# Turning the row maxima of an attention kernel with an fp32r product in place of an fp32 transpose

## The chip, the core and the metric

The kernel runs on one core of one Trainium2 chip. The time is the device time of one execution in microseconds (us); smaller is better. The engines of the core are TensorE (PE, with its weight loads shown apart as PEld), VectorE (DVE), ScalarE (ACT), GpSimd (POOL) and SyncE (SP), and each works through its own instructions in order.

## What is computed

A block of cross attention with 16 heads of width 64, followed by a mixture of 8 experts of which each token uses 2. The first argument of the attention (`x` inside it) is the context, 154 rows; the latents are the normalised `x`, 512 rows. The queries come from the latents, keys and values from both, 154 + 512 = 666 rows. Batch 2, width 128.

```python
def _L0_xattn_ref(x, latents, ln_m_g, ln_m_b, ln_l_g, ln_l_b, Wq, Wkv, Wout):
    x = layer_norm(x, ln_m_g, ln_m_b)
    lat = layer_norm(latents, ln_l_g, ln_l_b)
    q = lat @ Wq
    kv = jnp.concatenate([x, lat], axis=1) @ Wkv
    k, v = jnp.split(kv, 2, axis=-1)            # then split into 16 heads
    dots = jnp.einsum('bhid,bhjd->bhij', q, k) * scale
    attn = jax.nn.softmax(dots, axis=-1)
    out = jnp.einsum('bhij,bhjd->bhid', attn, v)
    return out @ Wout

x = x + _L0_xattn_ref(ctx_1024, _layernorm(x), ...)
x = x + _L0_ffn_ref(_layernorm(x), ...)         # 8 experts, top 2, hidden 256
```

## The kernel before

The order of all work is written out by hand, engine by engine, and semaphores tie the engines together. All operands live in the core's own memory; only weights are loaded on the way.

**Steps.** Attention runs in 16 steps `s`, one for each pair of heads and batch. The scores are held transposed: keys on the partitions (6 tiles of 111 keys, `kt` = 0 to 5), queries along the 512 columns. The softmax needs for each query the maximum over its keys, and this is found a step ahead on scores that are the other way round: `lead` makes them (queries on the partitions), `reduce_max` on VectorE takes the negated maxima of each of six units, and `join_max` joins them into `neg_max`, 2 heads of `TURN` = 64 columns, of which the first four of each head are used and the rest stay zero. `neg_max` is thus a tile of 128 by 128, with a query on each partition.

**The turn.** `turn_max` (line 343) turns this tile on TensorE: `neg_max` is the stationary operand and the identity `ident` streams through, 128 columns. The result stands in a bank of `sc`. `spread_max` on VectorE (line 782) multiplies it by a selection `sel` and writes `max_row` in fp32r; the last two products of each score tile (line 368) multiply `max_row` by ones, which subtracts the maximum from the scores. ScalarE then takes the exponential (`exponent`, line 636).

**Order on TensorE in a step** (lines 466 to 504): six rounds of `dots(s, kt)` (lines 362 and 368) with `lead_next(s + 1, kt)` behind each (line 326); the projections of q and k for step s + 2; half of a projection of v (`project_v`, lines 295 to 297, 9 products of 256 columns); `turn_max(s + 1)`; `total(s - 1)`, the softmax sums of the step before (line 389); and 24 records of `pv(s, kt)` (line 382). Step 14 has a part of the output projection (`out_project`, line 460) where the others have that of v, and step 0 has no `total`. `turn_max(0)` runs once ahead of the steps, behind the first half of `project_v(0)`.

**fp32 and fp32r.** An operand declared fp32r has 32 bits but is rounded to fewer digits by whoever writes it. Products of such operands stand in the trace as one record; ordinary fp32 products (lines 382, 389, 460, 564) stand there as two. The transposes of fp32 tiles (lines 345, 407, 410, 513, 530) stand there as one record. The trace prints both types as f32 on TensorE.

**GpSimd** builds `ident` and `sel` at the start (lines 972 to 987), then waits for the variances of the inputs (`rstd_of`, line 1000); in the steps it adds the exponentials up (`gather`, line 1050).

Of the kernel before, what the change touches and what calls it, by code (L numbers as in the profile page):

```python
# [15 lines left out]
F32 = mybir.dt.float32  # L16
F32R = mybir.dt.float32r
# [4 lines left out]
P = 128  # L22
# [19 lines left out]
TURN = 64  # L42
# [27 lines left out]
def xattn_moe(nc, x, ctx_in, g_m, b_m, g_l, b_l, wq, wkv, wout, wg, w1, b1, w2, b2, out):  # L70
    with ExitStack() as stack:
        def sb(name, shape, dt=F32):
            return stack.enter_context(nc.sbuf_tensor(name, shape, dt))
# [4 lines left out]
        def sem(name):  # L78
            return stack.enter_context(nc.semaphore(name))
# [4 lines left out]
        rows = sb("rows", [E * HC + 4, P])  # L84
        cols = sb("cols", [P, E * HC + 4])
        ident = sb("ident", [P, P])
        sel = sb("sel", [P, QT])
        sel2 = sb("sel2", [P, 2, QT])
        ones = sb("ones", [P, HD])
# [18 lines left out]
        k_pair = sb("k_pair", [P, QKB, 2, J], F32R)  # L108
        v_sb = sb("v_sb", [P, 2, KT, 2 * P])
        part_max = sb("part_max", [P, 2, 2, QT])  # L110
        neg_max = sb("neg_max", [P, 2, TURN])
        max_row = sb("max_row", [P, 2, N], F32R)
        probs = sb("probs", [P, RING, 2, N])
        psum_acc = sb("psum_acc", [P, 2, 2, N])
# [40 lines left out]
        tail_loaded = sem("tail_loaded")  # L155
        consts = sem("consts")
        sel_ready = sem("sel_ready")
        ones_ready = sem("ones_ready")
        cols_turned = sem("cols_turned")
        cols_ready = sem("cols_ready")  # L160
# [30 lines left out]
        neg_turned = sem("neg_turned")  # L191
# [101 lines left out]
        def _(pe):  # L293
# [48 lines left out]

            def turn_max(n, bank=sc[:, 1, 1, :]):
                pe.wait_ge(neg_ready, n + 1)
                pe.transpose(bank[:, 0:P], neg_max[:, :, :].rearrange("p h c -> p (h c)"), ident[:, :]) \
                  .then_inc(neg_turned, 1)

            def dots(s, kt):
                if kt == 0:
# [99 lines left out]
            pe.wait_ge(kv_ready, 2 * B)  # L449
            project_v(0, 0, sc[:, 0])  # L450
            turn_max(0, mx[:, 0, :])
            pe.wait_ge(v_copied, 1)

# [12 lines left out]
            for s in range(STEPS - 1):  # L466
# [21 lines left out]
                if v_half(s):  # L488
# [5 lines left out]
                    else:  # L494
                        project_v(*v_half(s))
                pe.wait_ge(exp_done, s * KT + KT)
                turn_max(s + 1)
                if s >= 1:
                    total(s - 1)
# [227 lines left out]
        def _(dve):  # L727
            own = [0]

            def chained(op):  # L730
                op.then_inc(setup_v, 1)
                own[0] += 1
                dve.wait_ge(setup_v, own[0])
# [62 lines left out]
                dve.reciprocal(at, at).then_inc(recip_done, 1)  # L796

            chained(dve.memset(moments[:, :, :, :], 1.0))
            dve.memset(neg_max[:, :, :], 0.0)

            def input_tiles(b):
                return [(t, x_tok[:, b, t, :]) for t in range(QT)] + \
# [168 lines left out]
        def _(pool):  # L971
# [13 lines left out]

            pool.wait_ge(consts, 3)
            pool.tensor_tensor(sel[:, :], sel2[:, 0, :], sel2[:, 1, :], ALU.add).then_inc(sel_ready, 1)

            def split_qk(p):
                pool.wait_ge(wqk_loaded[p % 2], 32 * (p // 2 + 1))  # L990
                if p >= 2:
                    pool.wait_ge(k_lo_done, 2 * (4 * (p // 2 - 1) + p % 2 + 2) + 2)
                pool.tensor_copy(wqk_hi[:, p % 2, :, :], wqk_raw[:, p % 2, :, :]).then_inc(wqk_hi_ready, 1)
                pool.wait_ge(wqk_hi_ready, p)
                pool.tensor_tensor(wqk_lo[:, p % 2, :, :], wqk_raw[:, p % 2, :, :],
                                   wqk_hi[:, p % 2, :, :].bitcast(F32), ALU.subtract).then_inc(wqk_split, 1)
# [114 lines left out]
```

## Time and profile before

| | us |
|---|---|
| median of 3 runs | 356.56 (356.44 to 356.78) |
| the profiled execution | 356.89 |
| its span, first to last instruction | 355.1 |
| TensorE busy | 342.6 (96%) |
| VectorE, GpSimd, ScalarE busy | 240.2, 240.7, 181.2 |

The span is what the trace covers; the profiled execution lasted 1.8 us longer than its span. TensorE's records overlap: the next product starts while one drains, so that the time a product costs is read from the start of one record to the start of the next, not from its duration. The weight loads (PEld) run ahead of the products that use them.

### The profile page before, as it was taken

The page shows a single profiled execution, that of the slowest core. Times are in us where ns is not written, and L with a number is a line of the kernel's source. Part 1 is how long each engine was busy: PE and PEld are TensorE (multiplying, and loading weights), DVE is VectorE, ACT ScalarE, POOL GpSimd, SP SyncE. Part 2 cuts the span into 40 slices and gives each one's busy share as a digit, 9 for nine tenths or more (in the row PEclk, how much of TensorE's full clock was granted, in tenths as well). Part 3 has the DMA queues.
Part 4 walks back from the last instruction along what each step waited for, and adds up shares of the span by engine and source line. Part 5 has one row for each costly group of instructions (what it writes and reads, how often), then busy time and mean ns, then how long its engine had stood idle before and what let it go on. Part 6 is the DMA issues. An engine that isn't in the chain of part 4 may idle for free.

```text
span 355.1 us, 6060 instructions
## 1 busy us (share of the span) xinstructions
PE 342.6 (96%) x2343; PEld 231.0 (65%) x2343; DVE 240.2 (68%) x418; ACT 181.2 (51%) x240; POOL 240.7 (68%) x160
## 2 busy tenths in 40 slices
PE   2879999999999999999999999999999999999996
PEld 2758574656657474756556474747584559999986
DVE  4789286878677686868686776968744488257433
ACT  2247383755648383836556383838433553135341
POOL 3577586979797989999798989779695661010000
PEclk9999999999999999999999999999999999999999
DMA  3044000000001010010100000000000000000000
GB/s 122 0 145 124 2 14 2 2 2 0 2 0 31 0 31 15 2 30 2 30 3 16 0 2 2 0 2 0 2 0 2 1 0 3 2 0 2 30 2 30
DMA packets 6713, 5.81 MB, mean 16 GB/s; under 512 B 743, under 2 KB 5789, under 8 KB 6685
## 3 DMA queue, kind: packets, MB, share of 16 engines
q1 hardware_dynamic: 6389, 5.29, 5.0%
q8 instruction: 19, 0.31, 0.3%
q10 hardware_dynamic: 296, 0.13, 0.1%
q14 instruction: 9, 0.07, 0.1%
HBM read 4.89 MB, written 0.52 MB: 15 GB/s over the span
## 4 chain that ended last, share of the span: by engine, by line
PE 94%; DVE 3%; DMA 1%; ACT 1%; ACTq 1%; issue 0%; DVEq 0%
PE xo L382 23%; PE sc L362 20%; PE mx L564 8%; PE sc L368 6%; PE sc L295 5%; PE xo L389 5%; PE sc L297 4%; PE sc L296 4%; PE mx L326 3%; PE xo L326 3%; PE mx L460 2%; PE xo L460 2%; PE mx L295 2%; PE mx L297 2%; PE mx L296 2%; DVE part_max L767 1%
## 5 line engine op out<-in xcount | busy, mean ns | idle before, releaser
L1050 POOL TENSOR_TENSOR psum_acc<-psum_acc,probs 111x1024 f32<-111x1024 f32 x63 | 150.0, 2380 | 7.2 <-DVE psum_acc L790 2.5
L636 ACT ACTIVATE probs<-sc 111x1024 f32<-111x1024 f32 x96 | 98.3, 1027 | 21.3 <-PE sc L368 13.9
L362 PE MATMUL sc<-q_pair,k_pair 64*111 64x512 f32 x576 | 85.7, 401 | 1.0 <-ACT v_sb L626 0.8
L382 PE MATMUL xo<-probs,v_sb 111*64 111x512 f32 x384 | 85.6, 593 | 0.0
L362 PEld LDWEIGHTS sc<-q_pair,k_pair 64*111 64x111 f32 x576 | 44.6, 170 | 28.4 <-issue 12.2
L767 DVE TENSOR_REDUCE part_max<-mx 128x2 f32<-128x888 f32 x32 | 34.7, 1084 | 41.0 <-PE mx L326 39.6
L382 PEld LDWEIGHTS xo<-probs,v_sb 111*64 111x64 f32 x384 | 27.3, 137 | 53.6 <-issue 53.2
L796 DVE RECIPROCAL recips<-recips 128x128 f32<-128x128 f32 x64 | 54.3, 910 | 9.4 <-ACT recips L646 9.4
L1050 POOL TENSOR_TENSOR psum_acc<-probs 111x1024 f32<-111x1024 f32 x16 | 38.4, 2398 | 30.7 <-ACT probs L636 30.7
L640 ACT COPY o_t<-xo 128x512 f32<-128x512 f32 x16 | 9.4, 588 | 66.6 <-PE xo L382 66.6
L368 PE MATMUL sc<-max_row,ones_r 64*111 64x512 f32 x192 | 38.1, 390 | 0.0
L703 ACT ACTIVATE probs<-sc,cols 128x512 f32<-128x512 f32 x32 | 21.5, 687 | 28.3 <-PE sc L297 28.0
L767 DVE TENSOR_REDUCE part_max<-xo 128x2 f32<-128x888 f32 x30 | 32.5, 1084 | 1.4
L941 DVE SCALAR_TENSOR_TENSOR x_tok<-mx,score,x_tok 128x128 f32<-128x128 f32 x62 | 17.5, 344 | 22.1 <-PE mx L564 21.9
L564 PEld LDWEIGHTS mx<-w_sb,probs 128*128 128x128 f32 x248 | 29.9, 192 | 2.0 <-issue 0.8
L564 PE MATMUL mx<-w_sb,probs 128*128 128x128 f32 x248 | 30.2, 275 | 0.0
L1057 POOL TENSOR_TENSOR o_t<-o_t,recips 128x512 f32<-128x512 f32 x16 | 20.5, 1278 | 11.2 <-DVE recips L796 11.2
L368 PEld LDWEIGHTS sc<-max_row,ones_r 64*111 64x111 f32 x192 | 16.9, 170 | 5.5
L326 PE MATMUL mx<-k_pair,q_pair 64*128 64x444 f32 (+1 forms) x128 | 18.3, 320 | 1.3 <-DVE part_max L767 0.5
L771 DVE TENSOR_REDUCE part_max<-mx 128x4 f32<-128x888 f32 x16 | 17.3, 1082 | 1.4
L626 ACT COPY v_sb<-mx 111x768 f32<-111x768 f32 x15 | 12.0, 799 | 12.0 <-PE mx L297 12.0
L389 PE MATMUL xo<-psum_acc,ones 111*64 111x512 f32 x64 | 17.3, 618 | 0.0
(169 smaller groups left out, 478.9 us busy)
## 6 DMA issues: line engine op xcount, KB each, us to landing
w_raw<-in_L_ffn_W SPq DMA_DIRECT2D x8, 128.0 KB, 2.0
x_tok<-in_x SPq DMA_DIRECT2D x2, 256.0 KB, 3.4
wv_raw<-in_L_xattn_Wkv SPq DMA_DIRECT2D x4, 128.0 KB, 2.8
wout_sb<-in_L_xattn_Wout SPq DMA_DIRECT2D x1, 512.0 KB
wqk_raw<-in_L_xattn_Wq SPq DMA_DIRECT2D x7, 64.0 KB, 2.0
wqk_raw<-in_L_xattn_Wkv SPq DMA_DIRECT2D x7, 64.0 KB, 2.0
out<-x_tok SPq DMA_DIRECT2D x1, 256.0 KB, 2.0
out<-x_tok SPq DMA_DIRECT2D x2, 128.0 KB, 1.7
```

Of the source, the lines that this page charges most:

```text
L295: pe.matmul(out_ap, st_hi, mv_hi, start=True, stop=False)
L326: mm = pe.matmul(to, q_pair[r, n % QKB, 0, t * P:(t + 1) * P], k_pair[r, n % QKB, 0, k_cols(u >= QT)], start=True, stop=True)
L362: pe.matmul(sc[0:KP, kt % 2, h, :], k_pair[r, s % QKB, k_part, at], q_pair[r, s % QKB, q_part, :], start=(k_part + q_part == 0), stop=False)
L368: mm = pe.matmul(sc[0:KP, kt % 2, h, :], ones_r[r, :], max_row[r, s % 2, :], start=False, stop=True)
L382: mm = pe.matmul(o_ps[h * HD:(h + 1) * HD, :], v_sb[0:KP, s // 2 % 2, kt, at:at + HD], probs[0:KP, e % RING, h, :], start=(kt == 0), stop= ...
L389: mm = pe.matmul(bank[h * HD:(h + 1) * HD, :], ones[0:KP, :], psum_acc[0:KP, s % 2, h, :], start=True, stop=True)
L564: mm = pe.matmul(y_ps(g, t)[:, t * P:(t + 1) * P], relu_ring[:, (g * HC + c) % FR, t * P:(t + 1) * P], w2_sb[:, e * HC + c, :], start=(c = ...
L636: act.activation(probs[0:KP, e % RING, :, :], sc[0:KP, kt % 2, :, :], ACT.Exp).then_inc(exp_done, 1)
L703: act.activation(relu_ring[:, n % FR, :], hid_ps[:, n % 4, :], ACT.Relu, bias=cols[:, n % (E * HC):n % (E * HC) + 1]).then_inc(relu_done, 1)
L767: dve.tensor_reduce(part_max[:, 0, :, u], banks[:, :, 0:KW], AX.X, ALU.max, negate=True) \
L796: dve.reciprocal(at, at).then_inc(recip_done, 1)
L1050: pool.tensor_tensor(psum_acc[0:KP, s % 2, :, :], first, probs[0:KP, e % RING, :, :], ALU.add) \
```

## The change

`neg_max` is declared fp32r, a copy `ident_r` of the identity in fp32r is made by GpSimd at the start, and `turn_max` becomes a plain product of the two. The first turn also waits for `ident_ready`. VectorE's clearing of `neg_max` writes the same bits through an fp32 view. No instruction changes its place; GpSimd gets one more.

```diff
@@ -84,6 +84,7 @@
         ident = sb("ident", [P, P])
+        ident_r = sb("ident_r", [P, P], F32R)
@@ -108,7 +109,7 @@
-        neg_max = sb("neg_max", [P, 2, TURN])
+        neg_max = sb("neg_max", [P, 2, TURN], F32R)
@@ -342,8 +344,10 @@
             def turn_max(n, bank=sc[:, 1, 1, :]):
                 pe.wait_ge(neg_ready, n + 1)
-                pe.transpose(bank[:, 0:P], neg_max[:, :, :].rearrange("p h c -> p (h c)"), ident[:, :]) \
-                  .then_inc(neg_turned, 1)
+                if n == 0:
+                    pe.wait_ge(ident_ready, 1)
+                pe.matmul(bank[:, 0:P], neg_max[:, :, :].rearrange("p h c -> p (h c)"), ident_r[:, :],
+                          start=True, stop=True).then_inc(neg_turned, 1)
@@ -796,7 +800,7 @@
-            dve.memset(neg_max[:, :, :], 0.0)
+            dve.memset(neg_max[:, :, :].bitcast(F32), 0.0)
@@ -985,6 +989,7 @@
             pool.tensor_tensor(sel[:, :], sel2[:, 0, :], sel2[:, 1, :], ALU.add).then_inc(sel_ready, 1)
+            pool.tensor_copy(ident_r[:, :], ident[:, :]).then_inc(ident_ready, 1)
```

## Rows read from the trace of the kernel before

**Rows 1.** The page: busy time of each engine, and shares of the last chain.
```profile
PE 342.6 (96%) x2343; PEld 231.0 (65%) x2343; DVE 240.2 (68%) x418; ACT 181.2 (51%) x240; POOL 240.7 (68%) x160
...
PE 94%; DVE 3%; DMA 1%; ACT 1%; ACTq 1%; issue 0%; DVEq 0%
```
**Rows 2.** Timeline of TensorE around one turn: start us, us, engine, line, operation, xcount.
```profile
66.49 0.27 PE L295 MATMUL sc<-kv_hi,wqk_hi 128*128 128x222 f32 x1
66.60 0.27 PE L296 MATMUL sc<-kv_lo,wqk_hi 128*128 128x222 f32 x1
...
67.76 0.29 PE L297 MATMUL mx<-wv_hi,kv_lo 128*111 128x256 f32 x1
67.88 0.27 PE L345 MATMUL sc<-ident,neg_max 128*128 128x128 f32 x1
68.09 1.08 PE L389 MATMUL xo<-psum_acc,ones 111*64 111x512 f32 x4
69.00 5.32 PE L382 MATMUL xo<-probs,v_sb 111*64 111x512 f32 x24
74.25 0.95 PE L362 MATMUL sc<-q_pair,k_pair 64*111 64x512 f32 x6
```
**Rows 3.** Line 345: its loads and products, ns min/median/max, and who waited for them.
```profile
L345 PEld LDWEIGHTS sc<-ident,neg_max x15: 138/140/144, 34.8 to 265.4; 128*128 128x128 f32 x15
L345 PE MATMUL sc<-ident,neg_max x15: 270/272/274, 34.9 to 265.6; 128*128 128x128 f32 x15
...
  DVE max_row L782: 9.0, 16
```
**Rows 4.** Waits of the whole span: engine, line, releaser: us in total, times, longest.
```profile
ACT o_t L640 <- PE xo L382: 66.6, 16, 4.6
...
DVE part_max L767 <- PE mx L326: 39.6, 15, 7.0
POOL psum_acc L1050 <- ACT probs L636: 30.7, 16, 4.3
...
PEld sc L362 <- ACT probs L636: 7.2, 36, 0.6
```
**Rows 5.** Timeline: a v product of 256 columns, then the 64-wide tiles of line 382.
```profile
38.84 0.28 PE L297 MATMUL mx<-wv_hi,kv_lo 128*111 128x256 f32 x1
39.05 0.20 PEld L382 LDWEIGHTS xo<-probs,v_sb 111*64 111x64 f32 x4
39.05 0.65 PE L382 MATMUL xo<-probs,v_sb 111*64 111x512 f32 x2
```
**Rows 6.** Timeline: an expert's product of 512 columns, then line 389.
```profile
290.74 0.40 PE L297 MATMUL sc<-kv_hi,w_lo 128*128 128x512 f32 x1
...
291.06 0.65 PE L389 MATMUL xo<-psum_acc,ones 111*64 111x512 f32 x2
```
**Rows 7.** Timeline: a transpose of 77 columns, then the half-height tiles of line 326.
```profile
20.77 0.23 PE L410 MATMUL sc<-ident,normed 77*128 77x77 f32 x1
20.92 0.37 PE L326 MATMUL sc<-k_pair,q_pair 64*128 64x222 f32 x2
```
**Rows 8.** Timeline: 128-column loads and products of 8 columns, eight of each.
```profile
287.18 0.97 PEld L521 LDWEIGHTS mx<-wg_sb,kv_t 128*128 128x128 f32 x8 [0.81 <-ACT kv_t L697]
287.18 1.06 PE L521 MATMUL mx<-wg_sb,kv_t 128*128 128x8 f32 x8
```
**Rows 9.** Timeline of the weight loads: fp32r loads of 128 columns at 222-column products.
```profile
14.99 0.19 PEld L296 LDWEIGHTS sc<-kv_lo,wqk_hi 128*128 128x128 f32 x1
15.10 0.19 PEld L297 LDWEIGHTS sc<-kv_hi,wqk_lo 128*128 128x128 f32 x1
```
**Rows 10.** Timeline: the join of the maxima, and the load and spread that use it.
```profile
66.33 0.17 DVE L777 TENSOR_REDUCE neg_max<-part_max 128x8 f32<-128x16 f32 x1
...
68.19 0.69 DVE L782 TENSOR_TENSOR max_row<-sc,sel 128x512 fp32r<-128x512 f32 x1 [0.25 <-PE sc L345]
...
67.76 0.14 PEld L345 LDWEIGHTS sc<-ident,neg_max 128*128 128x128 f32 x1
```
**Rows 11.** Timeline of the first turn.
```profile
23.31 0.27 PE L345 MATMUL mx<-ident,neg_max 128*128 128x128 f32 x1
23.51 0.80 ACT L626 COPY v_sb<-sc 111x768 f32<-111x768 f32 x1 [0.77 <-PE sc L297]
23.69 0.69 DVE L782 TENSOR_TENSOR max_row<-mx,sel 128x512 fp32r<-128x512 f32 x1 [0.78 <-PE mx L345]
...
24.36 0.71 PE L362 MATMUL sc<-q_pair,k_pair 64*111 64x512 f32 x4 [0.78 <-ACT v_sb L626]
```
**Rows 12.** Timeline of GpSimd at the start, and the group of its 256-column casts.
```profile
2.19 0.20 POOL L987 TENSOR_TENSOR sel<-sel 128x4 f32<-128x4 f32 x1
6.99 1.34 POOL L1000 TENSOR_TENSOR rstd<-var_eps,half_power 128x6 f32<-128x6 f32 x1 [4.59 <-DVE var_eps L808]
...
L993 POOL CAST wqk_hi<-wqk_raw 128x256 fp32r<-128x256 f32 x7 | 2.8, 399 | 2.2 <-DVE normed L746 2.2
```
**Rows 13.** The chain that ended last, in order of time: start us, us, what.
```profile
348.76 1.80 PE mx L564 x16
350.56 0.02 issue
350.58 1.14 DVE x_tok L941 x4
```

More of the change, by code:

```diff
@@ L157, in xattn_moe @@
         sel_ready = sem("sel_ready")
+        ident_ready = sem("ident_ready")
         ones_ready = sem("ones_ready")
```

## The prediction

> **What bounds the kernel now.** I read the page's shares first: TensorE is busy for 96% of the span and makes 94% of the chain that ended last, so a step is worth what it takes of TensorE's time from start to start, if the rest follows [rows 1]. Does it follow? In the waits, the long ones all point at TensorE or at something it drives: ScalarE waits 66.6 us for line 382, VectorE 39.6 us for line 326, GpSimd 30.7 us for the exponentials, each about once a step [rows 4]. No engine is full in a step and none keeps a pace of its own. TensorE's own waits inside the steps are the 36 short ones for exponentials, 7.2 us together [rows 4]; they are waits for a ScalarE that itself started from TensorE's scores, so they move with it. Behind the turn I see no wait at all: line 389 follows the turn at once, its 4 records and the 24 of line 382 run through to the next step's scores at 74.25 [rows 2]. At the end, TensorE works until 350.56 and VectorE adds up behind it [rows 13]. So time taken off a turn in a step should come off the end, one for one.
>
> The turn itself: line 345 is one record a turn, 15 in the steps and one ahead of them, 272 ns long with a load of 140 ns [rows 3]. What it costs is not 272 ns. It starts at 67.88 and line 389 starts at 68.09 (the same place of other steps gives 0.20): 0.20 us [rows 2]. That is the term of the sum, 15 times 0.20 us = 3.0 us, under 1% of the kernel, and the change can only take a part of it.
>
> **What the 0.20 us is made of.** The next product loads 64-wide tiles where the turn used the full array, and its load starts only with it. Every such switch in the trace shows the streaming of the last product plus about 0.1 us. A 256-column v product (fp32r) before line 382: 39.05 - 38.84 = 0.21 [rows 5]. A 512-column one before line 389: 291.06 - 290.74 = 0.32 [rows 6]. The difference is 0.11 us for 256 columns, 0.43 ns a column, and leaves 0.10 us for the switch. An fp32 transpose of 77 columns before another switch: 20.92 - 20.77 = 0.15 [rows 7]; with the turn's 0.20 at 128 columns that makes 0.05 us for 51 columns, some 0.8 to 1 ns a column. So a transposed fp32 column costs about twice an fp32r column, and the switch costs about the same 0.1 us behind both.
>
> **The change, part by part.** The product: 128 columns at 0.43 ns are 0.055 us, plus 0.10 for the switch: 0.155 us from the turn to line 389 where it was 0.20. Bounds: going down from the 512-column row, 0.32 - 384 x 0.42 ns = 0.16, with rounding 0.165; going from the 77-column transpose, whose stream was about 0.065, 0.15 - 0.065 + 0.055 = 0.14. So 0.045 us a turn, between 0.035 and 0.06. I take the middle because the 256-column row is nearest in kind: the same engine mode before, the same 64-wide fp32 tiles behind.
>
> No row has an fp32r product narrower than 222 columns. Those start 66.60 - 66.49 = 0.11 us apart [rows 2], which is still 0.43 ns a column and some 10 ns; whether 128 columns keep that rate is the unknown of this case.
>
> The load: a transpose loads 128 columns in 0.14 us [rows 3], an fp32r product in 0.19 [rows 9], 0.05 longer. Eight loads of 128 columns with products of only 8 columns start in 0.97 us, that is (0.97 - 0.19) / 7 = 0.11 us apart [rows 8], so such a load needs 0.11 us of the array's load path. It starts with the product before, which streams 256 columns and holds the turn back by 67.88 - 67.76 = 0.12 us anyway [rows 2]. The 222-column products hold loads of this size with 0.11 between them [rows 2, 9]. I cost it at nothing; the cover is that v product (in step 14 the output projection's last), and without it up to 0.05 us a turn would come back.
>
> The trace shows a transpose as a single record, and not as the two of an ordinary fp32 product, so the turn had no fourfold cost to lose. The Trainium skill says the same against this change ("TensorE: Matmul & The Clock Gate", Terms): transpose mode is 4x faster for FP32. By that rule the old turn would already stream at the fp32r rate and the change would gain nothing; rows 2 and 7, with 0.8 to 1 ns a column, say it is about half that fast, which no other row contradicts. It is the first rival below.
>
> The join on VectorE writes 8 fp32r elements instead of 8 fp32 ones. It ends at 66.50 and the load that needs it starts at 67.76 [rows 10]: 1.26 us of cover, and the other steps look alike. The spread starts about 0.04 us earlier, and nothing waits for that: its result is needed in the next step's line 368, over 5 us later [rows 2, 10].
>
> The first turn: behind it TensorE waits for ScalarE's copy of v, which ends at 24.31, and not for the turn [rows 11]. Gain and cost there: nothing. Its additional wait is for a copy on GpSimd at about 2.4 us. That copy is 128 columns, less than the 0.40 us of a 256-column cast, say 0.3; GpSimd then waited 4.59 us for VectorE's variances, so it is hidden too [rows 12]. The first turn comes at 23.31, so the wait is long fulfilled.
>
> **The sum.** 15 turns x 0.045 = 0.68 us; with the bounds 0.5 to 0.9. The profiled execution lasted 356.89, 0.33 over the median; the gain is a difference and carries over: 356.56 - 0.68 = 355.88. The three runs shown spread over 0.34 us. About 0.2% of this time, 0.71 us, is what a measurement can tell from no change, so the forecast lies just inside it, and its upper half outside.
>
> **The rivals.**
>
> *Nothing comes back (0.20).* Either the transpose already streams as fast as fp32r, or the longer load shows: 0.045 gained and up to 0.05 lost, or the gain is caught by a wait of ScalarE or GpSimd later in the step. Each gives 0 to 0.35 us, 356.2 to 356.6. Against: rows 7 against 2 for the rate, rows 8 for the load, rows 4 for the waits. For: 0.01 us of rounding in rows from which 0.045 is taken. The Trainium skill's section on the back-to-back gap (the same page) gives about 81 ns for a pair of load and 128-column product, as an estimate 0.03 us more than streaming alone; by it 0.02 us a turn and 0.3 us in all are gained.
>
> *Slower (0.10).* The fp32r rate does not hold for narrow products. If a product below some width between 128 and 222 columns falls back to what an ordinary fp32 one takes, it costs as two records of line 564: 16 records took 1.80 us [rows 13], 0.11 each, 0.22 for the product. From turn to line 389 that is 0.32 instead of 0.20, 15 x 0.12 = 1.8 us, time 358.4. The 222-column products show no sign of such a fall, which is why it gets little. It decides as soon as a 128-column stream costs over 0.10 us, what the transpose pays now. Half a fall, two cycles a column, would be no change.
>
> *More than the sum (0.05).* The switch is shorter behind an fp32r stream of this width, or a wait for exponentials goes too: 1.0 us or more, 355.5 or less.
>
> **Chances.** The forecast case, 0.5 to 0.9 us, has 0.65: of it 0.34 shows as faster by over 0.2% and 0.31 as within, since the sum lies just inside the bound and the medians scatter by 0.1 us or so. With the large gain faster has 0.39; with the first rival within has 0.51; slower has 0.10. The range goes from 355.6, the upper bound of the gain with some scatter, to 356.6, no gain at all; left out are the slow rival and a part of the large gain.
>
> **What would show it.** In the changed kernel's timeline the turn should start 0.12 behind the v product as before, and line 389 (393 in the changed file) 0.15 to 0.16 behind the turn; the product's duration falls from 272 to about 230 ns, its load rises from 140 to about 190. The distance between two turns, 16.2 us, should fall by 0.045. If the turn starts later behind the v product, the load shows. If the gap is 0.3, narrow fp32r products are slow. If the gap falls but the distance of turns doesn't, a wait in the scores' rounds took it.

## The result and the profile after

| | before | after |
|---|---|---|
| median, us (22 runs each) | 356.63 (356.37 to 357.10) | 356.19 (355.83 to 356.51) |
| profiled execution, us | 356.89 | 356.11 |
| its span, us | 355.1 | 354.4 |

The ratio is 0.9986, with a 95% interval from 0.9980 to 0.9992: 0.44 us or 0.14% less, a gain by its interval, and under the 0.2% that the prediction took as the least that a measurement can tell. In us the interval is 0.29 to 0.71. The forecast was 355.9 in a range from 355.6 to 356.6. In some executions of either kernel, though in none of these 44, TensorE's granted clock falls for a while near the start and the time is 1 to 2 us longer (last section); medians called "at full clock" below leave those out.

The turn in the changed kernel, in the timeline of TensorE (start us, us, engine, line, operation, xcount), answers to [rows 2]:

```profile
67.40 0.28 PE L299 MATMUL mx<-wv_hi,kv_lo 128*111 128x256 f32 x1
67.52 0.22 PE L349 MATMUL sc<-ident_r,neg_max 128*128 128x128 f32 x1
67.67 0.65 PE L393 MATMUL xo<-psum_acc,ones 111*64 111x512 f32 x2
```

It starts 0.12 us behind the v product, as it did, and line 393 (389 before) starts 0.15 behind it where it was 0.20. The instructions of the new line, with min/median/max in ns and the first and last start, answer to [rows 3]:

```profile
L349 PEld LDWEIGHTS sc<-ident_r,neg_max x15: 187/188/192, 34.4 to 264.7; 128*128 128x128 f32 x15
L349 PE MATMUL sc<-ident_r,neg_max x15: 218/221/305, 34.6 to 264.7; 128*128 128x128 f32 x15
...
  DVE max_row L786: 8.1, 16
```

The load is 0.05 us longer and the product 0.05 us shorter, about as forecast. The starts tell where the time went: in the timeline, from the second turn to the sixteenth it is 264.73 - 34.55 = 230.18 us, against 265.56 - 34.87 = 230.69 before. That is 14 steps, and 0.51 us less.

The busy time and the waits say nothing new, which is a result too; they answer to [rows 1] and [rows 4]:

```profile
PE 341.0 (96%) x2343; PEld 231.9 (65%) x2343; DVE 240.1 (68%) x418; ACT 181.3 (51%) x240; POOL 241.1 (68%) x161
...
ACT o_t L644 <- PE xo L386: 66.6, 16, 4.6
...
DVE part_max L771 <- PE mx L328: 39.5, 15, 7.0
POOL psum_acc L1055 <- ACT probs L640: 30.0, 16, 4.2
```

The copy of the identity, 0.29 us, sits in GpSimd's idle time at the start, and the join writes fp32r in the 171 ns that it took before (the first two rows are from the timeline, the last from the groups by shape; they answer to [rows 10, 12]):

```profile
2.34 0.29 POOL L992 CAST ident_r<-ident 128x128 fp32r<-128x128 f32 x1
7.08 1.34 POOL L1005 TENSOR_TENSOR rstd<-var_eps,half_power 128x6 f32<-128x6 f32 x1 [4.45 <-DVE var_eps L812]
...
L781 DVE TENSOR_REDUCE neg_max<-part_max 128x8 fp32r<-128x16 f32 x16 | 2.7, 171 | 0.6
```

So the turns gave 15 x 0.05 = 0.75 us, and 0.44 arrived by the medians. The upper end of the interval, 0.71, is close to 0.75, so the times alone don't prove that anything is missing; the steps of the trace do, for this one execution (next section). The question for the experiments was where that part stayed, and whether it is the narrow fp32r product, the type or the mode that makes a turn cheap.

### The profile page after: what moved, and what is told of

Its sections match the earlier page's. It is cut to its first block, busy times and chain, and to the rows that moved or that the text cites. A ratio compares the mean times of both kernels' runs of the same rounds, so it can differ in the third digit from the quotient of the medians.

```text
span 354.4 us, 6062 instructions
## 1 busy us (share of the span) xinstructions
PE 341.0 (96%) x2343; PEld 231.9 (65%) x2343; DVE 240.1 (68%) x418; ACT 181.3 (51%) x240; POOL 241.1 (68%) x161
## 4 chain that ended last, share of the span: by engine, by line
PE 92%; DVE 4%; ACT 1%; DMA 1%; ACTq 1%; issue 0%; DVEq 0%
PE xo L386 23%; PE sc L366 20%; PE mx L568 8%; PE sc L372 6%; PE sc L297 5%; PE xo L393 5%; PE sc L299 4%; PE sc L298 4%; PE mx L328 3%; PE xo L328 3%; PE mx L464 2%; PE xo L464 2%; PE mx L297 2%; PE mx L298 2%; PE mx L299 2%; DVE part_max L771 1%
## 5 line engine op out<-in xcount | busy, mean ns | idle before, releaser
L640 ACT ACTIVATE probs<-sc 111x1024 f32<-111x1024 f32 x96 | 98.3, 1027 | 21.6 <-PE sc L372 14.8
```

Source lines behind the costliest of these rows:

```text
L640: act.activation(probs[0:KP, e % RING, :, :], sc[0:KP, kt % 2, :, :], ACT.Exp).then_inc(exp_done, 1)
```

## A measure for the steps

The gain per step is 0.05 us, and single executions of one kernel lie up to 0.7 us apart. The trace is finer: from the turn to the sums it is 200 to 204 ns in each of the eleven steps used here of the kernel before. Whole steps differ more (16211 to 16272 ns in the same trace), so their mean carries some 5 ns of scatter (from their spread, an estimate). For each kernel I took the mean over the eleven steps from the third turn to the fourteenth, in which the work is the same, and split it: from the turn to the sums or, where the turn is several records, from the first of them; the rounds of the scores, numbered from 0 as `kt` is, each from its first product to that of the next round; the whole step. Two of the rounds are shown. In ns:

| kernel | turn to sums | round 2 | round 4 | step |
|---|---|---|---|---|
| before | 202 | 1181 | 1178 | 16235 |
| changed, the profile above | 150 | 1193 | 1202 | 16205 |
| changed again (e6) | 150 | 1175 | 1190 | 16188 |
| changed again (e12) | 149 | 1177 | 1188 | 16186 |
| all but the product (e3) | 202 | 1180 | 1179 | 16236 |
| transpose of fp32r data (e5) | 151 | 1177 | 1175 | 16178 |
| the same again (e11) | 151 | 1180 | 1177 | 16178 |
| 192 columns (e7) | 178 | 1182 | 1186 | 16231 |
| 256 columns (e1) | 207 | 1179 | 1181 | 16242 |
| 512 columns (e8) | 320 | 1178 | 1182 | 16357 |
| plain fp32 product (e4) | 313 | 1176 | 1184 | 16344 |
| four fp32r products (e9) | 485 | 1179 | 1197 | 16525 |
| four fp32r transposes (e10) | 385 | 1179 | 1188 | 16428 |

The piece from the sums to the first round is 6159 ns in every row. In the changed kernel's first profile rounds 2 and 4 are 12 and 24 ns longer than before and round 3 is 9 ns shorter, 27 ns in all; small differences elsewhere bring that to the 22 ns that are missing between the 52 ns off the turn and the 30 ns off the step. Rounds 2 and 4 are those which TensorE starts soonest behind the exponential that frees their bank: about 0.10 us behind its end, and 0.15 us in rounds 3 and 5.

## The experiments

**e1 and e8: a longer turn.** The changed kernel with a wider identity, whose further columns are zeros and write columns that nobody reads; every turn but the first streams 256 or 512 columns. In the diffs from here on, `...` stands for what is cut; here GpSimd's clearing of the further columns, and the wait of the first turn for it, are cut too.

```diff
-        ident_r = sb("ident_r", [P, P], F32R)
+        ident_r = sb("ident_r", [P, 256], F32R)          # or 512, 192
-                pe.matmul(bank[:, 0:P], neg_max..., ident_r[:, :],
+                wide = 256 if n else P
+                pe.matmul(bank[:, 0:wide], neg_max..., ident_r[:, 0:wide],
```

For 256 columns:

> The changed kernel, but from step 0's turn on the fp32r identity is 256 columns wide (the upper 128 are zeros and write columns nobody reads), so that the turn streams as long as an fp32 transpose should. From turn to line 389 0.21 us where the changed kernel has 0.15. Theory A (whatever a turn costs more or less reaches the end one for one): 15 x 0.055 = 0.8 us over the changed kernel, 357.0 us. Theory B (about a third of it is taken back by the rounds of the scores, as in the changed kernel, where 0.75 us came off the turns and 0.44 us off the time): 0.5 us over it, 356.7 us, no difference from the kernel before.

Measured: median 356.90 against 356.74 for before on the same chip, ratio 1.0005 (0.9988 to 1.0023); the interval holds both theories. For 512 columns there are two entries. In the first, six executions took 877.83, 1203.34, 360.59, 358.39, 358.44 and 358.79 us. The profiled one is the 877.83, so its trace isn't used here (last section); the 360.59 has the clock's fall of that section too, and the last three are at full clock and lie nearer to theory A's 358.7 than to 357.9.

> The same with 512 columns. From turn to line 389 0.32 us, 0.17 more than in the changed kernel, 15 times: 2.5 us. Theory A (one for one): 358.7 us. Theory B (two thirds arrive): 357.9 us. It also shows whether the rate of 0.43 ns a column holds from 128 to 512 columns.

The second was made for the trace:

> The 512-column identity again, since the execution that was profiled the first time was a disturbed one. From turn to line 389 0.32 us. Theory A (one for one above the changed kernel's 0.15): step 16.205 + 0.17 = 16.375 us; if a third is taken back, 16.32. Theory C: 16.35 to 16.37, because the kernel with plain fp32 products, 0.11 us longer than before, has passed on 0.11 of it.

Its time was 358.66, 1.65 over the 357.01 of before on that chip. The turn in the timeline, for 256 and then for 512 columns:

```profile
51.13 0.28 PE L350 MATMUL sc<-ident_r,neg_max 128*128 128x256 f32 x1
51.34 1.08 PE L394 MATMUL xo<-psum_acc,ones 111*64 111x512 f32 x4
```

```profile
51.74 0.40 PE L350 MATMUL sc<-ident_r,neg_max 128*128 128x512 f32 x1
52.06 1.08 PE L394 MATMUL xo<-psum_acc,ones 111*64 111x512 f32 x4
```

0.21 and 0.32 us to the next product, with 0.15 at 128 columns: (0.32 - 0.15) / 384 = 0.44 ns a column and 0.09 us for the switch. That is the line that the prediction had drawn from 256 and 512 columns, and it holds down to 128. On the path: the 512-column turn is 118 ns longer than the transpose and the step is 122 longer; 5 ns and 7 with 256 columns. Measured from the kernel before, everything arrives where a turn gets longer. Against theory B it is the 512 columns that speak: by it the step should be 16.32 us, and it is 16.357; theory A, drawn from the 16.205 of the changed kernel's first profile, had 16.375, and theory C's 16.35 to 16.37 holds it. e1 can't decide: its turn is as long as that of before, so theory B has the step of before for it, which came (16242 against 16235).

**e7: 192 columns**, the same edit.

> The identity is 192 columns wide: 0.18 us from turn to line 389, halfway. Theory A (the rounds of the scores take back a third of what the turn gives): step 16.22 us. Theory C (how much they take back depends on how TensorE's two half-array streams happen to meet, and not on the turn's length in order): anything from 16.19 to 16.24, off the line between the changed kernel's 16.205 and the 256-column one's 16.242.

The turn took 0.178 us as expected; the step 16231, only 4 ns under before although the turn was 24 shorter. This is off the line between 16205 and 16242 by 7 ns and within theory C's 16.19 to 16.24 us, a range that little could have missed. And it isn't in the rounds that the time stayed: they are 6 ns longer than before in all, and the stretch from the start of the last round to the turn is 13 ns longer (4048 against 4035). Its single time (358.65) is from an execution in which the clock fell near the start (last section), and says nothing on the steps.

**e3: all but the product.** fp32r `neg_max`, the copied identity and the additional wait, but the transpose as before.

```diff
-                pe.matmul(bank[:, 0:P], neg_max..., ident_r[:, :], start=True, stop=True)
+                pe.transpose(bank[:, 0:P], neg_max...bitcast(F32), ident[:, :])
```

> All of the change except the product: neg_max is written as fp32r, the identity is copied, the first turn waits for it, but the turn is the fp32 transpose as before, reading neg_max through an fp32 view. If the copy, the wait and the type cost nothing, this is the kernel before, 356.6 us within 0.2. If they cost the 0.3 us that are missing between the 0.75 us off the turns and the 0.44 us off the time, it is 356.9.

Median 356.87 against 356.74, ratio 1.0001 (0.9984 to 1.0017), and a step of 16236 against 16235 ns. Its turn reads as that of before:

```profile
L349 PEld LDWEIGHTS sc<-ident,neg_max x15: 137/140/143, 34.7 to 265.3; 128*128 128x128 f32 x15
L349 PE MATMUL sc<-ident,neg_max x15: 270/272/274, 34.8 to 265.4; 128*128 128x128 f32 x15
```

So the copy, the wait and the type cost nothing in the steps. The times could not have told: their interval reaches 0.6 us to either side. It is the trace that clears the three, since the changed kernel's loss is in the steps.

**e4: a plain fp32 product.** The kernel before with `pe.matmul` on the fp32 operands.

```diff
-                pe.transpose(bank[:, 0:P], neg_max..., ident[:, :])
+                pe.matmul(bank[:, 0:P], neg_max..., ident[:, :], start=True, stop=True)
```

> The kernel before, with a plain fp32 product in place of the transpose: two records of 0.11 us each should stand where one stood. From the first of them to line 389 0.11 + 0.20 = 0.31 us, 0.11 more than before, 1.65 us in all: 358.3 us one for one, 357.7 if only two thirds arrive. This is the price that an ordinary fp32 product would have had, and that narrow fp32r products would have had if they fell back to it.

```profile
53.32 0.38 PE L345 MATMUL sc<-ident,neg_max 128*128 128x128 f32 x2
53.64 0.65 PE L389 MATMUL xo<-psum_acc,ones 111*64 111x512 f32 x2
```

Two records, 0.32 us to the next product, a step 109 ns longer, median 358.59 against 356.74: 1.85 us more, ratio 1.0057 (1.0040 to 1.0073). All of the longer turn arrives again. The slow rival had named 358.4 for it, and the changed kernel is nowhere near that.

**e6 and e12: the changed kernel again.**

> The changed kernel once more, beside the others of this chip: 0.3 to 0.6 us under the kernel before, and 0.15 us from turn to line 389. In its trace the steps should be 16.20 to 16.21 us apart where before has 16.24, with rounds 2 and 4 of the scores some 0.01 and 0.02 us longer than before. If that lengthening was chance of one execution, the steps are 16.18 us apart, the full 0.05 less.

> The changed kernel a third time, for the comparison with the one above. 0.3 to 0.8 us under the kernel before. In its trace rounds 2 and 4 of the scores tell whether the time taken back is the kernel's (12 and 24 ns longer again) or the execution's (another pair of numbers).

In e6 the median was 356.06 against 357.01 (ratio 0.9961, 0.9946 to 0.9976); in e12 355.97 against 356.91. Four of the twelve times of e12 lie at 357.9 to 358.1, with the clock's fall of the last section; with them its ratio is 0.9991 (0.9975 to 1.0007), and the other eight lie between 355.69 and 356.15. At full clock the medians are 356.06 against 356.98 and 355.92 against 356.90. Both gains, 0.92 and 0.98 us, are larger than the 0.3 to 0.6 and 0.3 to 0.8 that I had expected. In both traces the step is 16.19 us, 47 and 49 ns less than before, so that nearly all of the 52 arrive. In e12 rounds 2 and 4 are 4 ns shorter and 10 longer than before, in e6 6 shorter and 12 longer. The first profile's 12 and 24 did not come back as a pair: round 2 is not longer here, and round 4 by half as much.

From the second turn to the sixteenth it was in e6:

```profile
L349 PEld LDWEIGHTS sc<-ident_r,neg_max x15: 187/189/192, 36.7 to 266.6; 128*128 128x128 f32 x15
L349 PE MATMUL sc<-ident_r,neg_max x15: 218/221/307, 36.8 to 266.6; 128*128 128x128 f32 x15
```

In the timeline the two starts are 36.78 and 266.64: 229.86 us, 0.83 less than before. Some 0.08 of it is how the last start is recorded: that turn stands behind an fp32 product, its start is recorded 31 ns behind that product's and its record is about 0.3 us long, with line 393 then 0.235 behind it, where 0.15 would be the turn's own share. The same holds for the first profile. Corrected for this, the 14 steps gave 0.75 us in e6 and 0.43 there.

**e5 and e11: a transpose of fp32r data.** The operands of the changed kernel, the mode of the kernel before.

```diff
-                pe.matmul(bank[:, 0:P], neg_max..., ident_r[:, :], start=True, stop=True)
+                pe.transpose(bank[:, 0:P].bitcast(F32R), neg_max..., ident_r[:, :])
```

> The changed kernel with its fp32r operands, but the turn is a transpose again, of fp32r data. It tells whether the type or the mode sets the cost. Theory A (the mode sets it: a transpose streams a column in twice the time, whatever 4-byte type it moves, and loads in 0.14 us): 0.20 us from turn to line 389, 356.7 us as before. Theory B (the type sets it): stream as in the changed kernel, 0.15 us, with the short load of 0.14: 356.2 us, as the changed kernel.

> The transpose of fp32r data once more, beside the changed kernel of this chip. Its load is hidden as well as the product's, so the median should be within 0.1% of the changed kernel's, and both 0.4 to 0.8 us under the kernel before. If the short load helps beyond the turn (the rounds of the scores were evener in its trace, steps 16.18 us apart), it is 0.2 to 0.4 us under the changed kernel.

```profile
L349 PEld LDWEIGHTS sc<-ident_r,neg_max x15: 138/141/143, 34.7 to 264.6; 128*128 128x128 f32 x15
L349 PE MATMUL sc<-ident_r,neg_max x15: 218/221/302, 34.8 to 264.6; 128*128 128x128 f32 x15
```

The product's duration is that of the changed kernel, 221 ns, and the load's is that of the transpose, 141: the type sets the stream, the mode sets the load. The turn takes 151 ns to the sums. The step is 16178 ns in both executions, 57 less than before: all of the 51 ns arrive. Medians: 355.75 against 357.01 (0.9956, 0.9941 to 0.9972) and 355.84 against 356.91 (0.9966, 0.9953 to 0.9978). Beside the changed kernel of the same chips it is 0.31 and 0.13 us less; the intervals overlap on the first chip, and on the second the medians at full clock are 355.80 and 355.92, with times from 355.52 to 356.33. These are 1.26 and 1.07 us under the kernel before; for e11 I had expected 0.4 to 0.8. One of the eleven executions of e11 took 573.76 us (last section). So this version has the shortest steps seen, by 8 ns over the better traces of the changed kernel, and its lead in time is not shown.

**e9 and e10: four turns in a row**, as product and as transpose, from the second turn on. It measures the load where no wide product covers it.

```diff
+                for _ in range(3 if n else 0):
+                    pe.matmul(bank[:, 0:P], neg_max..., ident_r[:, :], start=True, stop=True)
                 pe.matmul(bank[:, 0:P], neg_max..., ident_r[:, :], start=True, stop=True)
```

> The changed kernel with every turn but the first done four times in a row, so that the second to fourth have no 256-column product ahead of them to cover their loads. Theory of the prediction (a 128-column fp32r load takes 0.11 us of the load path, hidden only by what streams before it): the four start 0.11 us apart, although each streams only 0.055; an added turn costs 0.11 us, 15 x 3 x 0.11 = 5.0 us in all. Rival (loads of this size hide behind any product): 0.06 us apart, 2.6 us.

> The same with four transposes of fp32r data. If the short load of a transpose (0.14 us as recorded, where the product's takes 0.19) is half as long on the load path, and the stream is that of fp32r, they start 0.055 to 0.06 us apart: 15 x 3 x 0.058 = 2.6 us more. If the load is no shorter in truth, 0.11.

First the four products, then the four transposes; line 350 is the three added turns and line 352 the last:

```profile
52.40 0.45 PE L350 MATMUL sc<-ident_r,neg_max 128*128 128x128 f32 x3
52.69 0.27 PE L352 MATMUL sc<-ident_r,neg_max 128*128 128x128 f32 x1
52.89 0.65 PE L396 MATMUL xo<-psum_acc,ones 111*64 111x512 f32 x2
```

```profile
51.39 0.37 PE L350 MATMUL sc<-ident_r,neg_max 128*128 128x128 f32 x3
51.59 0.25 PE L352 MATMUL sc<-ident_r,neg_max 128*128 128x128 f32 x1
51.77 1.08 PE L396 MATMUL xo<-psum_acc,ones 111*64 111x512 f32 x4
```

The loads of the four products, in the timeline of the weight loads:

```profile
52.29 0.41 PEld L350 LDWEIGHTS sc<-ident_r,neg_max 128*128 128x128 f32 x3
52.62 0.19 PEld L352 LDWEIGHTS sc<-ident_r,neg_max 128*128 128x128 f32 x1
```

The products take 0.49 us from the first to line 396, 0.34 more than one alone: 0.11 for each added turn, though it streams only 0.055. The loads are 0.11 us apart as expected. The starts of the products are not: they are 0.058, 0.111 and 0.113 apart, and line 396 starts 0.20 behind the last, where one turn alone has 0.15. The records of the second to fourth are 0.27 us long instead of 0.22. Read together: a product's record starts when the one ahead has streamed, and the wait for its own load, 0.05 us here, stands inside the record. Only the sum over the group is to be read as its cost. The transposes take 0.38, 0.23 more than one alone: 0.08 each, less than the products but more than the 0.058 that I had expected. Their starts are 0.060, 0.065 and 0.085 apart, the last two records are 0.02 us longer, and the second to fourth load are about 0.09 apart, so that here too the load is the longer part. The times were 361.72 and 359.23 (one run each), 5.7 and 3.4 us over the medians of the single turns, 5.0 and 3.5 by 15 x 0.335 and 15 x 0.234.

So the load of a product is 0.11 us where nothing covers it. No run has the fp32 transpose without cover, but the kernel before has four such transposes in a row in its second half, (0.60 - 0.27) / 3 = 0.11 us apart:

```profile
318.70 0.60 PE L513 MATMUL xo<-ident,normed 128*128 128x128 f32 x4
```

That is as much as one of e9's products, so that by these rows the change would gain nothing in such a place: its 0.05 us exist because a 256-column product stands ahead of the turn. A transpose of fp32r data doesn't need that cover as much.

## Why the prediction was right

*The number.* 356.19 lies in the range, but the range goes up to no gain at all, so this says little. The gain of 0.44 us is under the forecast case of 0.5 to 0.9 us and just over the 0 to 0.35 of the first rival; on the two other chips it is over 0.9. That the time came out between the cases is in part luck; what bears the prediction out is the turn in the traces.

*What bounds the kernel.* Right. TensorE's path takes what the turn gives or costs: 118 ns more in the turn were 122 in the step, 111 were 109, and 51 less were 57 less. No other engine kept a pace of its own. The two exceptions are the first profile of the changed kernel (52 less, 30 arrived) and e7 (24 less, 4 arrived).

*The stream and the switch.* Right in kind, its gain a little low: 0.155 us from turn to line 389 had been forecast from rows of 256 and 512 columns, and 0.150 came. The unknown, whether narrow fp32r products keep the rate, is settled by e1, e7 and e8 for 128, 192, 256 and 512 columns. The term of the sum was 15 x 0.045 = 0.68 and measured 15 x 0.05 = 0.75 on the turns. For the transpose the prediction went by 77 and 128 columns in front of a switch; the four transposes of line 513, 0.11 us apart, give its rate more directly and agree, 0.85 ns a column.

*The load at nothing.* Right, and for the reason given: the turn starts 0.12 us behind the v product with the longer load as with the shorter one. e9 shows the price without the cover, 0.11 us a load. The last turn, the only one behind a product that isn't fp32r, comes to the same: from the output projection's last record to line 393 it is 31 + 235 = 266 ns, against 112 + 202 = 314 before.

*Join, copy, wait, first turn at nothing.* Right for the steps, by e3's trace as a whole. Its median is 0.13 us over that of before, inside the interval.

*One for one to the end.* This is the step that was too simple in the comparison: 0.44 us arrived, not 0.68. In the profile of that kernel 22 of the 52 ns of each step stayed, most of it in rounds 2 and 4. I first took that for a rule (a third is taken back). e8 and e4 refuted it for longer turns, and e6 and e12 for this kernel itself: the same code kept only 5 and 4 ns in two other executions. It is not a longer wait either, as the prediction's last sentence would have had it: the exponentials last the same to about 1 ns on average, and the time is inside the rounds, from the first product of a round to its last (768 ns in round 2 and 760 in round 4, against 750 and 739 before). In these rounds TensorE runs two half-array products at a time, and in the trace with the long rounds the first two of a round start 14 and 21 ns apart in rounds 2 and 4, against 9 and 5 in the trace of before. But e8 has 13 ns in round 2 with 750 from first to last, and e9 has 9 in round 4 with 758. So the distance within a pair doesn't account for the long rounds. What makes one execution's rounds longer than another's stays open, and no kernel here sets it.

*What a turned column costs.* The Trainium skill ("TensorE: Matmul & The Clock Gate", Terms) has transpose mode as 4x faster for FP32. e4 has the plain product at two records of 0.11 us and the transpose at one: a factor of 2 in time on TensorE's path, not 4. The other factor of 2 comes with the type, as e5 shows. The Trainium skill's section on the back-to-back gap (the same page) gives about 81 ns for a pair of load and product at 128 columns. e9 has 112 ns for fp32r products, e10 about 78 for fp32r transposes, and under the cover of the v product it is 55 plus the switch; the measured numbers decide.

What stays open is the size on one chip against another: 0.44 us in 22 runs of each, and 0.92 and 0.98 us at full clock in e6 and e12, outside the first one's interval. The traces of the latter, 15 x 0.048 = 0.72, lie between. Medians at full clock are 356.63, 356.65, 356.98 and 356.90 for the kernel before on four chips, and 356.19, 356.06 and 355.92 for the changed one. Single profiles can't settle it: even in those without a fall of the clock the second turn starts anywhere from 34.3 to 35.4 us, a spread larger than the whole gain.

## What to carry to other kernels

For a small product on TensorE, read the distance from its start to the start of what follows, and look for what stands ahead of it: the 128-column load of an fp32r product cost 0.11 us here unless the product ahead streamed that long, and a switch of the tile shape cost about 0.1 us on top of the last stream, behind fp32r products of 128 to 512 columns and behind fp32 transposes. Data that will be rounded to fp32r anyway can be turned as fp32r, which halved the stream; in transpose mode it kept the short load as well. When a change takes 0.05 us off a step, compare steps within traces of several executions before explaining a part that is missing: one trace gave 22 ns lost a step, two others 5 and 4.

## What the runs showed of the hardware that I had not expected

The start of the kernel has two forms. In most traces TensorE's granted clock is 1.00 throughout. In e6's profiled execution (358.03 us, where the median is 356.06) it fell between 18 and 30 us. The table of windows for before and then for e6 (window: length, PE busy and count, granted clock, DMA share, GB/s):

```profile
12.00:18.00 6.00, 5.01 (x28) 1.00 0.00 0
18.00:24.00 6.00, 4.68 (x32) 1.00 0.28 76
24.00:30.00 6.00, 5.28 (x44) 1.00 0.93 264
```

```profile
12.00:18.00 6.00, 4.84 (x27) 1.00 0.00 0
18.00:24.00 6.00, 5.12 (x31) 0.84 0.28 80
24.00:30.00 6.00, 5.22 (x30) 0.59 1.05 292
```

0.84 and 0.59 are means over windows in which the clock stood at 1.2 GHz for a part and at 2.4 for the rest. The second turn then started at 36.8 us instead of 34.6, about the whole difference of such a run. The traces of e4, e7 and e12 show the same start; the other traces have no fall, or no record of the clock (e2 and e8). What TensorE did ahead of it doesn't tell them apart: it was busy for 4.84 of 6 us in e6, where the clock fell, for 5.01 before and for 4.21 in the first profile of the changed kernel, where it didn't. What decides is not shown. By the mean clock of each run (0.99 or 0.995 with a fall; for the 22 of the kernel before in the first comparison, by the times) it was there in 4 of 23, 4 of 19, 1 of 22 and 0 of 22 executions of the kernel before, and in 0 of 22, 2 of 13 and 4 of 12 of the changed one, so it isn't the change's. At 1 to 2 us it costs more than this change gives.

Three executions were far longer: 573.76 us in e11, with a mean clock of 0.564, and 877.83 and 1203.34 us in e2. Of these only the 877.83 has a trace. Its products on line 367 (362 before) last 824 ns where they last 401 before, while ScalarE's exponentials last 1025 ns as ever (1027): TensorE alone ran at half its pace or less. The granted clock reads 1.00 for it, and its trace has no record of the clock, so whether that fell is not shown.

```profile
L387 PE MATMUL xo<-probs,v_sb 111*64 111x512 f32 x384 | 232.4, 1437 | 0.0
L367 PE MATMUL sc<-q_pair,k_pair 64*111 64x512 f32 x576 | 192.5, 824 | 0.7 <-ACT v_sb L631 0.7
```
